# A fused four-layer kernel on one core: GpSimd's order of scatters, fetches and state steps in the first layer

## What is computed

```
xn = layernorm(x)
x  = x + ssm(xn) + moe(xn)

ssm: chunks of 128 tokens, 64 heads of 8 values, state of 128 x (64*8)
  S_next = S * exp(sum of a over the chunk) + states     # state carried from chunk to chunk
  y      = Yd(within the chunk) + Yoff(from S) + D * xs
  out    = rmsnorm(y * silu(z)) * norm_w @ W_out
moe: 8 experts, each token goes to its 2 best; plus a shared expert for all tokens
  routed = sum over the 2 chosen of share * expert(xn)
```

## Time and profile before

| what | value |
|---|---|
| median of 3 runs | 1502.84 us (1494.15 to 1506.90) |
| the profiled execution's own time | 1498.83 us |
| its span, first to last instruction | 1497.1 us |
| mean granted TensorE clock | 0.938 of full speed |
| busy TensorE / VectorE / ScalarE / GpSimd | 1286.0 / 885.9 / 567.9 / 354.7 us |

### The profile page before, as it was taken

How to read it: one execution, slowest core, us unless ns; L and a number is a source line. 1 busy time by engine, 2 the same in 40 slices (tenths; PEclk the granted TensorE clock), 3 DMA queues, 4 the chain that set the end, 5 groups by cost and what they waited for, 6 DMA issues and landing times. The chain is left out here.

```text
span 1497.1 us, 21861 instructions
## 1 busy us (share of the span) xinstructions
PE 1286.0 (86%) x7439; PEld 804.8 (54%) x7443; DVE 885.9 (59%) x1723; ACT 567.9 (38%) x957; POOL 354.7 (24%) x344
## 2 busy tenths in 40 slices
PE   5677988998988687999999998999766989998987
PEld 3334646654664455666666644454543456544564
DVE  5767566556656585543224379889777453556334
ACT  2474476547647551222222242443312313223311
POOL 3186031221302522510301002221037000000045
PEclk9788999999999888999999999999857999999999
DMA  9142123122211412300000150000002100111123
GB/s 360 55 139 84 47 60 96 50 54 71 79 41 35 132 51 97 103 1 0 0 0 0 68 186 0 1 0 1 2 28 85 31 28 29 36 43 57 57 58 111
DMA packets 72082, 88.87 MB, mean 59 GB/s; under 512 B 19174, under 2 KB 55334, under 8 KB 71337
## 3 DMA queue, kind: packets, MB, share of 16 engines
q1 hardware_dynamic: 65836, 70.78, 15.1%
q0 software_dynamic: 6144, 16.79, 3.5%
HBM read 61.14 MB, written 26.38 MB: 58 GB/s over the span
## 5 line engine op out<-in xcount | busy, mean ns | idle before, releaser
L414 PE MATMUL l_banks<-l_xnT,all_region_a 128*128 128x512 f32 x288 | 133.7, 612 | 5.6 <-ACTq L805 4.8
L2019 PE MATMUL l_banks<-l_xnT,mid_region_c 128*128 128x512 f32 (+1 forms) x192 | 89.6, 617 | 10.8 <-DVE l_xnT L2235 10.8
L970 POOL TENSOR_TENSOR all_region_b<-all_region_b,l_lc 128x512 f32<-128x512 f32 x64 | 88.2, 1398 | 31.5 <-DMA all_region_b<-l_lc_rows 31.2
L414 PEld LDWEIGHTS l_banks<-l_xnT,all_region_a 128*128 128x128 f32 x288 | 55.0, 197 | 65.9 <-issue 55.5
L794 ACT ACTIVATE all_region_b<-all_region_b 128x512 f32<-128x512 f32 x64 | 69.5, 1087 | 17.9 <-PE l_banks L414 14.0
L414 PE MATMUL l_banks<-all_region_a,all_xa 128*128 x234 | 68.7, 411 | 6.9 <-DVE all_x L1041 5.4
L1200 DVE SCALAR_TENSOR_TENSOR l_xbc<-l_pre,all_cols,l_xbc 128x512 f32<-128x512 f32 x72 | 61.7, 857 | 19.2 <-ACT l_xbc L727 14.2
L2019 PEld LDWEIGHTS l_banks<-l_xnT,mid_region_c 128*128 128x128 f32 (+1 forms) x192 | 35.2, 189 | 57.3 <-issue 45.4
L962 POOL TENSOR_TENSOR l_yr<-l_yr,all_neg_half 128x1 f32<-128x1 f32 x16 | 10.3, 643 | 232.7 <-DVE l_yr L1063 232.7
L2902 POOL TENSOR_TENSOR l_rstd<-l_moments,all_neg_half 128x4 f32<-128x4 f32 x12 | 12.4, 1032 | 220.8 <-DVE l_moments L2962 220.8
L1257 DVE TENSOR_TENSOR all_region_b<-all_region_b,l_cbd 128x512 f32<-128x512 f32 x64 | 59.0, 924 | 7.6 <-ACT all_region_b L794 3.9
(11 more groups left out here) (475 smaller groups left out, 2854.6 us busy)
## 6 DMA issues: line engine op xcount, KB each, us to landing
all_region_b<-l_lc_rows SPq DMA_DIRECT2D x256, 64.0 KB, 2.0
all_xa<-slots_in SPq DMA_DIRECT2D x39, 128.0 KB, 2.1
slots_out<-all_xa SPq DMA_DIRECT2D x39, 128.0 KB, 2.1
mid_vector_rows<-slots_in SPq DMA_DIRECT2D x39, 128.0 KB, 2.1
slots_out<-all_region_a SPq DMA_DIRECT2D x39, 128.0 KB, 1.7
slots_in<-l_xp SPq DMA_DIRECT2D x4, 1024.0 KB, 12.8
all_region_a<-l_gate_up SPq DMA_DIRECT2D x1, 4096.0 KB, 15.8
all_x<-x SPq DMA_DIRECT2D x4, 512.0 KB, 5.7
```

Of the source, the lines that this page charges most:

```text
L414: return nc.tensor.matmul(out, lhsT, rhs, start=start, stop=stop, **kw)
L970: nc.gpsimd.tensor_tensor(bc[:, k, :, :], bc[:, k, :, :], spread(lc[:, c, heads], 1, BLK), ALU.subtract).then_inc(dd_ready.sem, 1)
L2019: return nc.tensor.matmul(out, lhsT, rhs, start=start, stop=stop)
```

## The change

GpSimd's program in the first layer is put in another order, and three steps of VectorE's in the last group move; no instruction is added or removed.

In the first group, before: scatter 4, 5 | fade 0 | differences 1 | scatter 6 | scatter 7, 8 | fade 1 | differences 2 | scatter 9, 10 | out_scale 0 | scatter 11, 12 | fade 2 | differences 3 | scatter 13, 14, 15 | out_scale 1. After: fade 0 | scatter 4 | differences 1 | scatter 5, 6, 7 | fade 1 | differences 2 | scatter 8 to 11 | out_scale 0 | fade 2 | differences 3 | scatter 12 to 15 | out_scale 1.

In chunk 1 of the last group, before: fetch 0 to 3 | fade 1 | differences 2 | out_scale 0. After: fade 1 | differences 2 | fetch 0 to 3 | out_scale 0.

On VectorE in the last group, add(0) and add(1) move from the middle of chunk 1 to its end, add(2) and add(3) from chunk 1 to the middle of chunk 2, and measure(0) from the end of chunk 1 to chunk 2.

```diff
-        late = {0: ((6,), (7, 8)), 1: ((9, 10), (11, 12)), 2: ((13, 14, 15), ())}
+        late = {0: ((4,), (5, 6, 7)), 1: ((), (8, 9, 10, 11)), 2: ((), (12, 13, 14, 15))}
         for g in range(GROUPS):
             if g == 0:
                 for t in range(GT):
                     scatter(t)
             differences(g, 0)
-            if g == 0:
-                for t in range(GT, GT + 2):
+            for c in range(NCH):
+                fade(g, c)
+                ahead, behind = late.get(c, ((), ())) if g == 0 else ((), ())
+                for t in ahead:
                     scatter(t)
-            for c in range(NCH):
+                if c + 1 < NCH:
+                    differences(g, c + 1)
+                for t in behind:
+                    scatter(t)
                 if (g, c) == (GROUPS - 1, 1):
                     for t in range(GT):
                         fetch(t)
-                fade(g, c)
-                ahead, behind = late.get(c, ((), ())) if g == 0 else ((), ())
-                if c + 1 < NCH:
-                    differences(g, c + 1)
-                    for t in ahead:
-                        scatter(t)
                 if c > 0:
                     out_scale(g, c - 1)
-                for t in behind:
-                    scatter(t)
...
                 near(g, c, 2)
                 tiles_and_unit(g, c, 1)
-                if (g, c) == (GROUPS - 1, 1):
-                    add(0)
-                    add(1)
+                if (g, c) == (GROUPS - 1, 2):
+                    add(2)
+                    add(3)
...
                 near(g, c, 3)
                 tiles_and_unit(g, c, 2)
-                if (g, c) == (GROUPS - 1, 1):
-                    add(2)
-                    add(3)
+                if (g, c) == (GROUPS - 1, 2):
+                    measure(0)
...
                 if c > 0:
                     out_stats(g, c - 1)
                 if (g, c) == (GROUPS - 1, 1):
-                    measure(0)
+                    add(0)
+                    add(1)
                 if (g, c) == (GROUPS - 1, 2):
                     thresholds()
```

## The result

The changed kernel takes 1486.3 us (median of 11 runs, 1480.5 to 1488.2), the kernel before 1497.5 us beside it (11 runs, 1494.2 to 1506.9). The ratio is 0.9906, 95% interval 0.989 to 0.9923: 14.1 us less, where the prediction said 16.3.

A forecast was written before the change was run, and what follows sets the result against it. No engine was taken to bound the last group's chunk 1: VectorE waits for GpSimd's fade behind eight fetches. Last group 12.4 plus first group 3.9 make 16.3 us off the median 1502.84: 1486.5, range 1482 to 1491 (8 in 10: 1478 to 1500).

The forecast's parts named there:

- within 1%: Whole kernel: the outcome that the time stays within 1% of the kernel before, chance 0.46.
- faster by over 1%: Whole kernel: the outcome of a gain over 15 us, chance 0.48.
- Building the chunk from its neighbour: Last group, chunk 1: length built from chunk 2, 16.25 us from y to out_stats plus adds; 17.1 us gained.
- Charged in full with 4.7 us: Last group, chunk 2: second pair of adds (2.19 + 0.46) and measuring (2.04) lengthen it from 21.52 to 26.2 us.
- rival 3: Last group, chunk 1: TensorE's clock stays at 0.76, or a later layer's clock falls; gain 0 to 8 us, chance 0.13.
- (c): First group, chunk 2: wait for the fade falls from 4.18 to 0.46 us, up to 3.6 more if the multiply shortens.
- 1: Late chunks: differences shut VectorE out as before, the multiply stays long; 2.6 us lost, gain 13.7, time 1489, chance 0.17.
- 2: Last group: fetches beside VectorE's work launch and land slower, up to 1.50 us each; gain 9.9, time 1493, chance 0.14.
- 4: Last group: first adds wait for fetched rows, everything behind them late; slower, 1518 us at worst; chance 0.06 with other slowdowns.

The follow-up runs named there:

- the tail edit: The changed kernel with add(2), add(3) and measure(0) moved from chunk 2 into chunk 3 of the last group: 1509.9 us, ratio 0.9944; again 1512.5 us, 0.995.

## Why the prediction was right

The forecast was a gain of 16.3 us; the ratio gives 14.1 and the two profiles 18.1, on either side of it. The 14.1 us lie a little under the forecast's own 14.5 to 19, and at 0.94% inside "within 1%", not in the "faster by over 1%" that was given the larger chance. That the time itself was met (1486.5 forecast, 1486.3 measured) is in part luck: the median of the kernel before came out at 1497.5 over 11 runs, and the forecast had started from 1502.84.

**Last group, chunk 1.** Predicted: y to y 19.0 us, wait 0.46, multiply 0.93, out_stats 16.25 after y and adds behind it without a wait. Measured: 19.13, 0.46, 0.93, 16.76 and none. Building the chunk from its neighbour gave the size to 0.15 us, with two terms that miss by more and cancel: 0.5 us too little up to out_stats, 0.4 too much behind it. The two halves of the change run alone leave a wait each, 5.8 us for fetched rows or 9.17 for the fade.

**Last group, chunk 2.** Charged in full with 4.7 us; it paid 4.3 (25.82 against 21.52). That nothing hides it was right: the tail edit took it away again, 21.3 us, though on the other kind of chip.

**Chunk 3.** No term for it. It took 15.30 instead of 13.82, at a clock of 0.89 instead of 1.00. This is rival 3's second half on a small scale, a lower clock behind the place of the gain, worth 1.5 us. What brings it isn't shown. In the changed kernel TensorE has stood idle more in chunk 2 (clock 0.87 instead of 1.00); but of six profiles on the slower kind that have chunk 2 at 21.3 to 21.5 us and a clock of 1.00, as before, two have chunk 3 at 13.82 us and 1.00 and four have it at 15.2 to 16.4 us and 0.89 to 0.79. 12.4 predicted for the group, 11.1 measured.

**First group.** Predicted 3.9; 5.3 measured by y 3, by other terms. Chunk 0 lost 1.8 instead of nothing: the first product on W_up ran 2.98 us instead of 1.98, at a granted clock of 0.66 instead of 0.99, so VectorE could go on at 95.65 instead of 94.31. Chunk 1 gained 3.9 where I had nothing: before, its fade was late (VectorE waited 2.19 us) and its multiply took 4.58; with a later y and scatters already gone the fade was on time, and the multiply took 0.93. The rows of the kernel before:

```profile
109.89 0.69 DVE L1274 TENSOR_TENSOR l_st<-l_st,l_banks 128x512 f32<-128x512 f32 x1 [2.19 <-POOL l_st L980]
110.72 4.58 DVE L1257 TENSOR_TENSOR all_region_b<-all_region_b,l_cbd 128x512 f32<-128x512 f32 x1
```

That is the same pair as in the other two places, and the prediction left it out because it counted the scatters ahead of the fade and not when they end. Chunk 2 gained 3.2, and what limits it was named rightly (the landing of the scatters, y predicted at 149.4, measured 148.04, the chunk itself beginning 2.05 us sooner). In (c) I gave the multiply as possibly short; it was long, and by the run without fetches that made no difference there. So 3.9 against 5.3 is near by luck: a loss and a gain that the sum did not have.

**Rivals.** 1 held in that one chunk only (the first group's chunk 2), covered by the scatters. 2: launches of 0.95 to 1.29 us beside VectorE's work instead of 0.94, landing in 3.1 us at the median instead of 4.3; GpSimd was free at 517.1, before it was wanted, so it did not hold. 3: its first half, a clock that stays low, did not hold in the result's profile (1.00 in chunk 1), but on the slower kind of chip chunk 1 had 0.80, and the gain was 3 us. 4 did not hold, and the run with GpSimd's order alone shows it at work (5.8 us) when the adds aren't moved.

**The rule of the Trainium skill** on the shared port (page "SBUF — State Buffer", section "Who interferes with whom") would have a late multiply wait for one of GpSimd's instructions. All fades straight behind launches with differences that run without a gap speak against it: 4.56 to 4.60 us in the kernel before, in the one with VectorE's moves alone, in the changed kernel's first group and in the run without fetches, the length of nearly all four differences.

**What the prediction did not have** is the chip. It would have been wrong on the other kind: 3 us there. It took TensorE's work beside the fetches at the length that it had without them, and on three of the four chips of the experiments that does not hold. There the last group's chunk 1 is 7.0 us longer than in the result (4.2 us more busy time of TensorE at a lower clock, 2.5 of idle rows), and the last group's first y comes 1.3 us sooner than in the kernel before instead of 6.9 (one profile of each). That indirect DMAs and the stalls belong together is argued from where the rows and the lost time stand, not shown by taking the DMAs away: the run made for that met a chip without stalls, so the cause stays open, and so does what differs between the chips.

## What to carry to other kernels

Size a moved wait by rebuilding the chunk from a neighbour that already has the wanted order, and then ask which work of the old chunk was done under the wait that goes: here both the adds and the fetches had been free there. Then count over all chunks that the work moves through: on the slower chips moving the adds shortened chunk 1 by 5.0 us and lengthened chunk 2 by 4.9. Displaced work belongs where its engine is idle (chunk 3, VectorE 45% busy), not in the next chunk. And a gain that moves DMA launches beside a stream of small matmuls should be timed on more than one chip.

## What the runs showed of the hardware

- The multiply takes 4.56 to 4.60 us where the fade ran straight behind launches and four differences followed without a gap (4.92 to 4.95 us in all), and 0.93 where GpSimd had stood idle before the fade and VectorE waited for it (5.4 to 6.0 us for the four). How late the fade was doesn't decide it: the long multiply came with waits of 0.32, 0.94, 2.19, 4.18 and 9.30 us. Where VectorE came later than an early fade (last group, chunk 2 of the changed kernel) it was 1.52, with 5.44 for the differences.
- The same kernel takes 1498 or 1520 us by the chip. Most of it is lost in three stretches with indirect DMAs (9.0, 11.3 and 4.1 us of 24.3), none in the 774 us between the last two, though layer 3's scatters are launched there. On the slower kind TensorE stands idle 0.2 to 0.9 us ahead of single matmuls, and ScalarE and VectorE wait up to 24.12 and 11.79 us, with no releaser that the profile knows. In the last group's chunk 1 (26.11 us instead of 19.13) the granted clock is 0.58 instead of 1.00 ahead of the first of those idle rows, behind 9.21 us that were alike.
- Eight fetches cost TensorE and VectorE nothing that can be measured on the faster kind: 19.13 us with them, 19.10 without.
